# Attention scores as 32x32 tiles of TensorE in four PSUM banks, in a kernel of layer norm, attention, GRU and feed-forward

## The reference

```python
x = x + attn(cond(x, ...))                 # cond: block sums, softmax over 8 blocks, layer norm
# attn: 32 heads of size 8, causal, with a slope on the distance
scores = einsum('bhqd,bhkd->bhqk', q, k) / sqrt(8)
probs  = softmax(where(causal, scores, -10000) + alibi * m)
attn   = einsum('bhqk,bhkd->bhqd', probs, v) @ W_proj + b_proj
x = x + ffn(gru(cond_2048, x, ...))        # 32 steps of a GRU over the tokens
```

## Time and profile before

| | |
|---|---|
| time, median of 3 runs | 455.13 us (454.35 to 455.9) |
| time of the profiled execution | 453.68 us |
| its span | 451.9 us |
| PE busy | 430.9 us, 95% |
| DVE busy | 326.4 us, 72% |
| ACT busy | 247.0 us, 55% |
| POOL busy | 109.6 us, 24% |

### The profile page before, as it was taken

One profiled execution on the slowest core, in us unless ns is written; L12 is line 12 of the kernel. 1 busy time (PEld: TensorE's weight loads), 2 busy tenths in 40 slices (PEclk: granted clock), 3 DMA queues, 4 the chain that ended last, 5 costly groups with the idle time before them and its releaser, 6 DMA issues.

```text
span 451.9 us, 13521 instructions
## 1 busy us (share of the span) xinstructions
PE 430.9 (95%) x5470; PEld 354.6 (78%) x5470; DVE 326.4 (72%) x1008; ACT 247.0 (55%) x564; POOL 109.6 (24%) x127
## 2 busy tenths in 40 slices
PE   8899799999999999999999889899999999999994
PEld 5657587786877777778677779799999999999984
DVE  3656688697888886988867955657676677667665
ACT  6255648558485585674866653444444444444341
POOL 7422345424344453341544310000000000000000
PEclk9999999999999999999999999999999999999999
DMA  7802512424134142321312200001010101000002
GB/s 299 317 4 80 166 34 82 136 71 144 36 91 133 47 120 75 95 82 38 99 26 61 60 3 2 0 2 46 1 49 0 48 5 45 25 23 25 23 25 70
DMA packets 34268, 30.36 MB, mean 67 GB/s; under 512 B 4128, under 2 KB 29344, under 8 KB 34208
## 3 DMA queue, kind: packets, MB, share of 16 engines
q1 hardware_dynamic: 34208, 29.51, 20.9%
HBM read 16.91 MB, written 8.39 MB: 56 GB/s over the span
## 4 chain that ended last, share of the span: by engine, by line
PE 74%; DVE 14%; ACT 4%; issue 3%; DMA 2%; POOL 2%; SPq 1%; DVEq 0%; POOLq 0%; ACTq 0%
PE ps_a L1089 10%; PE ps_s L1234 7%; PE ps_t L1234 6%; PE ps_o L1234 6%; PE ps_s L1288 5%; PE ps_s L1138 5%; PE ps_m L1180 5%; PE ps_t L1288 4%; PE ps_a L1288 4%; PE ps_t L1151 4%; PE ps_m L1288 4%; PE ps_o L1162 3%; DVE mx L822 2%; PE ps_m L1172 2%; PE ps_a L1036 2%
## 5 line engine op out<-in xcount | busy, mean ns | idle before, releaser
L475 POOL TENSOR_TENSOR sc<-masked,mx 128x512 f32<-128x512 f32 x32 | 45.8, 1431 | 111.0 <-DVE mx L822 111.0
L1089 PE MATMUL ps_a<-yT_r,w_qkv_r 128*128 128x512 f32 x192 | 50.2, 406 | 1.6 <-POOL yT_r L449 1.2
L814 DVE COPY_PREDICATED masked<-kst,ps_s 128x512 f32<-128x512 int32 x64 | 43.9, 734 | 2.3 <-PE ps_s L1138 2.0
L1089 PEld LDWEIGHTS ps_a<-yT_r,w_qkv_r 128*128 128x128 f32 x192 | 34.6, 189 | 11.9 <-POOL yT_r L449 2.1
L676 ACT ACTIVATE zg<-ps_t,brz 128x128 f32<-128x128 f32 x64 | 20.1, 365 | 39.6 <-PE ps_t L1234 37.4
L574 ACT ACTIVATE sc<-sc 128x512 f32<-128x512 f32 x64 | 37.1, 621 | 7.1 <-DVE sc L828 5.6
L822 DVE TENSOR_REDUCE mx<-masked 128x16 f32<-128x512 f32 x64 | 40.4, 671 | 0.0
L952 DVE SCALAR_TENSOR_TENSOR rg<-ps_o,vec,rg 128x128 f32<-128x128 f32 x64 | 19.5, 348 | 24.9 <-PE ps_o L1234 24.0
L506 ACT ACTIVATE pT<-ps_t 128x512 f32<-128x512 f32 x64 | 34.9, 602 | 4.1 <-PE ps_t L1151 3.2
L1234 PEld LDWEIGHTS ps_s<-hT,w_hh 128*128 128x128 f32 x256 | 33.0, 191 | 4.8 <-DVE hT L970 2.8
L1180 PE MATMUL ps_m<-oT,w_p 128*128 128x128 f32 x256 | 35.3, 281 | 0.8 <-ACT oT L506 0.8
(11 more groups left out here) (128 smaller groups left out, 869.9 us busy)
## 6 DMA issues: line engine op xcount, KB each, us to landing
xf<-in_x_feat SPq DMA_DIRECT2D x8, 512.0 KB, 4.1
xg<-in_x_tok SPq DMA_DIRECT2D x8, 512.0 KB, 4.9
kbd<-kn SPq DMA_DIRECT2D x128, 32.0 KB, 1.9
v_dram<-vn SPq DMA_DIRECT2D x16, 256.0 KB, 3.1
vbd<-v_dram SPq DMA_DIRECT2D x64, 64.0 KB, 2.0
out_feat<-ost SPq DMA_DIRECT2D x16, 256.0 KB, 2.0
w_qkv<-in_wqkv SPq DMA_DIRECT2D x1, 768.0 KB, 7.6
w_ih<-in_wih SPq DMA_DIRECT2D x1, 768.0 KB, 10.4
```

The lines of the kernel that those rows point to most:

```text
L475: nc.gpsimd.tensor_tensor(shifted, kept, m.unsqueeze(2).to_broadcast([P, NH // 2, S]), ALU.subtract).then_inc(sc_sub[1], 1)
L814: nc.vector.copy_predicated(kept, keep.unsqueeze(1).to_broadcast([P, NH // 2, S]), ps_s[:, h * 512:(h + 1) * 512].rearrange("p (h k) -> p ...
L1089: last = nc.tensor.matmul(bank, w_qkv_r[a][:, c, first_col + m * P:first_col + (m + 1) * P], yT_r[b][:, c, :], start=(a == b == c == 0), s ...
```

## The change

It sets `RH = 4`, and so `KH = 4`. The scores of a tile are then 32 matmuls on sixteen tiles of 32x32, four groups of rows by four of columns, each with 128 columns of output; the keys are block-diagonal over four heads instead of eight, and `kbd` is half as large. Each of the four row groups has a PSUM bank of its own and fills half of it: two banks of `ps_s`, and two of `ps_u`, which has the place of `ps_t`. The transposed probabilities now go to `ps_s`. So the scores of tile n + 1 and the transposed probabilities of tile n share two banks, and `transpose_probs(n)` has a new wait for DVE's masked copy of half 0 of tile n + 1. PE's order changes so that other work stands between the scores and the transposes, and in step 1 ACT's copy of the first query chunk moves ahead of `attn_out`. The diff, cut to its core:

```diff
-RH = 2
+RH = 4
 KH = P // RH // 8
-            return {"r": ps_s, "z": ps_t, "n": ps_a}[which][:, m * 512:(m + 1) * 512]
+            return {"r": ps_u, "z": ps_s, "n": ps_a}[which][:, m * 512:(m + 1) * 512]
+        def score_banks(h):
+            return (ps_s, ps_u)[h][:, :].rearrange("p (r x) -> p r x", r=RH // 2)[:, :, 0:C * KH * S]
# ACT, tile_step
+                if i == 1 and not last_group:
+                    q_chunk(g + 1, 0)
                 if n > 0:
                     attn_out(n - 1)
...
                 if i == 1 and not last_group:
-                    q_chunk(g + 1, 0)
                     q_chunk(g + 1, 1)
# DVE, softmax_mask
-                    nc.vector.copy_predicated(kept, keep.unsqueeze(1).to_broadcast([P, NH // 2, S]),
-                                              ps_s[:, h * 512:(h + 1) * 512].rearrange("p (h k) -> p h k", k=S)
-                                              ).then_inc(sc_out, 1)
+                    kept = masked[:, h * 512:(h + 1) * 512].rearrange("p (r h k) -> p r h k", r=RH // 2, k=S)
+                    nc.vector.copy_predicated(
+                        kept, keep.unsqueeze(1).unsqueeze(1).to_broadcast([P, RH // 2, C * KH, S]),
+                        score_banks(h).rearrange("p r (h k) -> p r h k", k=S)).then_inc(sc_out, 1)
# PE, scores
+                if n >= 2:
+                    pe.wait_ge(pt_out, 2 * n - 2)
                 for c in range(C):
                     for r in range(RH):
                         rows = slice(r * P // RH, (r + 1) * P // RH)
+                        bank = score_banks(r // 2)[:, r % 2, c * KH * S:(c + 1) * KH * S]
                         for b in range(TB):
                             cols = slice(i * P + b * S, i * P + (b + 1) * S)
-                            out_cols = slice((r * C + c) * KH * S, (r * C + c + 1) * KH * S)
-                            last = nc.tensor.matmul(ps_s[b * S:(b + 1) * S, out_cols], qn[rows, g % 2, c, cols],
+                            last = nc.tensor.matmul(bank[b * S:(b + 1) * S, :], qn[rows, g % 2, c, cols],
                                                     kbd[rows, c, :, cols], start=True, stop=True,
                                                     tile_position=(r * P // RH, b * S))
# PE, transpose_probs
+                if n + 1 < NT:
+                    pe.wait_ge(sc_out, 2 * n + 3)
+                else:
+                    pe.wait_ge(pt_out, 2 * n)
                 for h in range(2):
                     pe.wait_ge(sc_exp, 2 * n + h + 1)
-                    if not first:
-                        pe.wait_ge(pt_out, 2 * n - 1 + h)
                     for q in range(HW):
                         col = (h * HW + q) * P
-                        last = nc.tensor.transpose(ps_t[:, col:col + P], sc[:, p, col:col + P], ident)
+                        last = nc.tensor.transpose(ps_s[:, col:col + P], sc[:, p, col:col + P], ident)
                     last.then_inc(pt_mm, 1)
# PE, tile_step
+                products_ahead = g + 3 < NG and i == 3
+                if n + 1 < NT:
+                    scores(n + 1, (n + 1) // GT, (n + 1) % GT)
                 if i == 0 and not last_group:
                     transpose_y(g + 1, norm_ahead and g > 0)
-                if n + 1 < NT:
-                    scores(n + 1, (n + 1) // GT, (n + 1) % GT)
-                if n > 0:
-                    transpose_attn(n - 1)
+                if i == 1 and not last_group:
+                    work_ahead(g + 1, 1, 0)
                 if norm_ahead and i == 2:
                     pe.wait_ge(q_out, 2 * g + 4)
                     spread_proj(g + 2, ps_a)
-                transpose_probs(n, n % 2, first=(n == 0))
+                if products_ahead:
+                    pe.wait_ge(v_out, 2 * g + 4)
+                    block_product(g + 3, ps_a[:, 0:512], 0)
+                if n > 0:
+                    transpose_attn(n - 1)
+                transpose_probs(n, n % 2)
```

More of the change, by code:

```diff
@@ L172, in adaln_attn_gru_ffn @@
         ps_s = ctx.enter_context(nc.psum_tensor("ps_s", [P, 1024], F32))
-        ps_t = ctx.enter_context(nc.psum_tensor("ps_t", [P, 1024], F32))
+        ps_u = ctx.enter_context(nc.psum_tensor("ps_u", [P, 1024], F32))
         ps_o = ctx.enter_context(nc.psum_tensor("ps_o", [P, 512], F32))
@@ L580, in probs_out @@
                     copy_out(pT[:, h * HW:(h + 1) * HW, :].rearrange("p q n -> p (q n)"),
-                             ps_t[:, h * 512:(h + 1) * 512]).then_inc(pt_out, 1)
+                             ps_s[:, h * 512:(h + 1) * 512]).then_inc(pt_out, 1)
             def attn_out(n):
@@ L806, in softmax_mask @@
             def softmax_mask(n, p, first=False):
-                for h, kept, _, _ in halves(p):
+                for h in range(2):
                     if not first:
@@ L883, in _ @@
             rest_of_proj(1, proj_ps_1)
-            add_proj(1, ps_t)
+            add_proj(1, ps_u)
             token_stats(1)
@@ L1129, in scores @@
                 pe.wait_ge(q_out, C * (g + 1))
-                if not first:
+                if first:
+                    pe.wait_ge(z_done, 4)
+                else:
                     pe.wait_ge(sc_out, 2 * n)
+                if n >= 2:
+                    pe.wait_ge(pt_out, 2 * n - 2)
                 for c in range(C):
@@ L1213, in _ @@
             work_ahead(0, 1, 0)
-            spread_proj(1, ps_t)
+            spread_proj(1, ps_u)
             work_ahead(0, 1, 1)
@@ L1260, in tile_step @@
                     cond_row(g + 2)
+                if i in (0, 2) and not last_group:
+                    work_ahead(g + 1, i, 0)
                 if i < 3 and not last_group:
-                    work_ahead(g + 1, i, 0)
                     work_ahead(g + 1, i, 1)
-                if g + 3 < NG and i == 3:
-                    pe.wait_ge(v_out, 2 * g + 4)
-                    block_products(g + 3, ps_a[:, 0:512])
+                if products_ahead:
+                    block_product(g + 3, ps_a[:, 0:512], 1)
                 if norm_ahead and i == 1:
```

6 lines of the change are left out of this document (3 added, 3 removed).

## The result

The changed kernel takes **461.07 us** (median, 460.78 to 461.25) against 455.27 for the kernel before on the same chip: ratio 1.0128, 95% interval 1.011 to 1.0147. It is slower by 5.8 us, where 451.1 was forecast, and outside the range. The profiled execution has a span of 459.2 us against 451.9.

A forecast was written before the change was run, and what follows sets the result against it. Bound by PE, then DVE in steps 2 and 3, then ACT 0.11 behind PE. Terms -0.42 - 2.94 + 0.35 - 0.55 - 0.45 = -4.0 took 455.13 to 451.1 us; range 446.5 to 455.3.

The forecast's parts named there:

- the size of the score block: All score matmuls of one tile of tokens on PE: 0.60 us instead of 1.02, saving 0.42 a block.
- 0.73 is an upper bound on what the issue costs: Issue of 64 PE instructions in a score block: at most 0.73 us, taken from `probs_v`.
- Start: First scores, on the chain with DVE waiting for them: -0.42 us.
- Step 1: Groups 0 to 6, PE sets the step and the new wait is hidden by 0.17: seven times -0.42, -2.94 us.
- Steps 2 and 3: Scores to end of transposes: 9.95 us against 9.88, the moved block product filling the saving; five groups, +0.35.
- The rival with a block of 1.02: Sixteen tiles no faster than eight, new wait stays: step 3's transposes end at 10.58 us, total 459.0; chance 0.09.
- Step 3 into 0: Groups 0 to 4: ACT's list of 6.57 us sets the start of `project_out`; five times -0.11, -0.55 us.
- End: After the last value projection DVE sets the pace and loses its waits for scores: -0.45 us.
- SP: Key load queue: half as many loads let the save go up to 1.0 us earlier; counted as nothing.
- The masked copy: DVE's copy reading two banks keeps its 0.64 us; 0.1 more on DVE's part would cost 0.2 a group.
- third rival: Score block keeps 1.02 us on sixteen tiles and the new wait stays: +3.9, 459.0 us; chance 0.09.
- if PE's denser instructions arrive late: Sign that the forecast would be wrong, on PE's instruction supply; no size given.

The follow-up runs named there:

- e12: Kernel before, each score matmul cut in two of 128 columns, a tile taken up again only after the other seven: 458.89 us, ratio 1.0075.
- e6: Changed kernel, each score matmul reading 64 of its 128 key columns from the third tile on: 456.59 us (one run).
- e9: Changed kernel, each score matmul reading 32 of its 128 key columns from the third tile on: 455.91 us (one run).
- e8: Changed kernel, score block in two halves, one ahead of the earlier tile's `probs_v` and one behind it: 467.24 us, ratio 1.0255.
- e3: Changed kernel, `transpose_y`, half projection, `spread_proj` and block product moved ahead of the scores: 478.69 us, ratio 1.0502.
- e13: Changed kernel, tile order in a sweep turned, column groups outside and row groups inside: 461.47 us, ratio 1.0133.
- e14: Changed kernel, second sweep taking the row groups as 1, 0, 3, 2: 461.24 us, ratio 1.0121.
- e4: Changed kernel, half of the score matmuls left out from tile 2 on, so the output is not the reference's: 451.41 us, ratio 0.9913.
- e2n: Kernel before with the new order of PE and ACT alone, old tiles and banks, no new wait: 457.21 us, ratio 1.0057.
- e2: Kernel before with the new wait and the new order of PE and ACT, old 64x32 tiles and banks: 461.3 us, ratio 1.0117.
- e5: Kernel before, each score matmul cut into four of 64 columns, run one after the other on the same tile: 555.3 us (one run).
- e1: Kernel before with only the new wait for the next tile's masked copy ahead of the transposes: 470.77 us, ratio 1.0333.

## Why the prediction was wrong

**The step that failed is the size of the score block**: "I take 0.60, since its working reproduces the block of before", with the bound under it, "0.73 is an upper bound on what the issue costs". The block is 4 x 0.109 + 0.57, not + 0.16. The constant was read from eight tiles, where it is 0.16 with 16 matmuls (1.02 - 0.86) and 0.22 with 32 (e12), and carried over to sixteen. The bound is none either: `probs_v` runs on four tiles and with 40 columns. PE's timeline of a block of the changed kernel shows where the rest is:

```profile
128.88 0.34 PE L1148 MATMUL ps_s<-kbd,qn 32*32 32x128 f32 x8
128.94 0.34 PE L1148 MATMUL ps_u<-kbd,qn 32*32 32x128 f32 x8
129.00 0.34 PE L1148 MATMUL ps_s<-kbd,qn 32*32 32x128 f32 x8
129.07 0.32 PE L1148 MATMUL ps_u<-kbd,qn 32*32 32x128 f32 x8
129.18 0.52 PE L1148 MATMUL ps_s<-kbd,qn 32*32 32x128 f32 x9
129.43 0.29 PE L1148 MATMUL ps_u<-kbd,qn 32*32 32x128 f32 x1
129.43 0.27 PE L1148 MATMUL ps_s<-kbd,qn 32*32 32x128 f32 x1
129.44 0.29 PE L1148 MATMUL ps_u<-kbd,qn 32*32 32x128 f32 x1
...
129.54 0.40 PE L1148 MATMUL ps_u<-kbd,qn 32*32 32x128 f32 x9
```

The first four rows are the first sweep: sixteen tiles start in 0.12, some 7 ns apart, and all of them their second instruction in the next 0.13. The tiles do run side by side. Then comes the second sweep, and it is unlike the first. One by one in the trace: the 32nd start is at 0.246 from the block's first, the 33rd at 0.30, the 34th, that tile's second instruction, a full 0.11 later at 0.41; from there the first instructions of the other fifteen tiles come 16.6 ns apart, and their second ones between them (the alternation of ps_u and ps_s in the last rows). The last start is at 0.79 and the next instruction of PE at 0.99. In e6 and e9 the spacing is 16.6 ns too, with a half and a quarter of the columns. A pause of 0.16 and fifteen starts at 16.6 instead of 7 ns (0.14) are 0.30 of the 0.41 by which the constant was too small. In e8, where `probs_v` stands between the sweeps, both are like the first.

**Why a second sweep right behind the first is slower stays open.** It is not what stands ahead (e3), the order of the tiles or the reuse of one (e13, e14). What e12 does not exclude is the number of instructions in the block. Its starts within a sweep over eight tiles come 7 ns apart up to the 36th, and from the 37th on (0.48 from the first) mostly 17 ns apart, as here; on eight tiles that costs little, since a sweep lasts one pass of 0.109 anyway. Where a block has 32 instructions (before, e4, e8) no such spacing shows. In both kernels PE's weight loads halt behind the 33rd of the block's 64. Against this rival speaks `probs_v`, whose 64 instructions keep a mean spacing of 9.5 ns. No run separates a sweep over tiles taken up again from a long block.

TensorE: Matmul & The Clock Gate of the Trainium skill, Part 1, has about 25 ns between starts as a floor, however few columns a matmul has. With starts 7 ns apart on sixteen tiles the trace disagrees, as it did with `probs_v`.

Point by point:

- **Start, -0.42.** Came to +0.35 in these two traces: the first block of scores is 0.25 shorter for DVE but starts 0.60 later, 40.01 against 39.41. The later start is in part scatter: in PE's timeline it is at 39.94 here, at 39.38 in e9 and 39.34 before.
- **Step 1, -0.42 each.** +0.02. PE sets the step, and no wait shows in it, as reasoned; the saving was not there. In e4, with a block shorter by 0.56, it is 0.23, and the wait that was to be hidden takes part of the rest.
- **Steps 2 and 3, +0.07 each.** From step 2's scores to the end of step 3's transposes: 151.63 to 161.31 + 0.87 = 162.18, so 10.55 against 9.88, +0.67. The rival with a block of 1.02 had 10.58. The order alone (e2n) loses 0.57 here: with a block of 1.02 ahead of it, the moved block product makes PE the later one.
- **Step 3 into 0.** The 6.57 of ACT's list came out exactly, at 131.21 + 0.87 to 138.65. But it is no gain of 0.11 once the transposes themselves are later.
- **End, -0.45.** The last two groups lost 3.5. Of that the stop and the low clock behind it are 2.5 in the last two steps (6.85 and 4.38 where e2 has 4.68 and 4.02), if e2's are taken as what they would be without.
- **SP.** Eight issues in 10.82 us for sixteen in 13.09, and no wait for keys or values. Nothing, as counted.
- **The masked copy** from two banks takes 0.72 to 0.74, as in the earlier trace rows.

```profile
233.34 10.82 SPq L341 DMA_DIRECT2D kbd<-kn  x8
```

The third rival ("sixteen tiles are no faster than eight, and the new wait stays") is what happened in its block, steps and total: it said 459.0, and 461.1 less 2.5 is 458.6. The reason it gave for the block, that four groups of rows do not run side by side, is not what the timeline shows, so its 1.02 is right by luck. It had a chance of 0.09, too little. Against it I held that two row groups run side by side, which says nothing about a second sweep; and `probs_v` in 0.73 was the only row near the new form, 64 instructions on four tiles.

**The stop.** The prediction named it as a risk ("if PE's denser instructions arrive late") and gave it no price. In the timeline:

```profile
262.05 0.35 PE L1148 MATMUL ps_u<-kbd,qn 32*32 32x128 f32 x6
...
264.28 0.41 PE L1148 MATMUL ps_u<-kbd,qn 32*32 32x128 f32 x3 [1.88 <-issue]
...
265.76 1.79 PE L1193 MATMUL ps_m<-oT,w_p 128*128 128x128 f32 x8
267.49 1.30 PE L1175 MATMUL ps_o<-vbd,pT 128*32 128x40 f32 x64
```

Behind the stop, `project_out` and `probs_v` are slow as well, 1.79 and 1.30 where they take 1.06 and 0.80. That is the clock and not the code. PE had stood still from 262.40 to 264.28, and 1.6 us after it went on the granted clock fell to 1.2 GHz for 3.4 us. The row gives the stretch, its length, the busy time of PE, PEld, DVE, ACT and POOL, the granted clock, the DMA share and GB/s:

```profile
265.90:269.30 3.40, 2.88 (x73) 2.50 (x71) 2.64 (x7) 1.98 (x4) 1.43 (x1) 0.50 0.02 5
```

In the chain the two take 1.63 and 1.27 there, against 0.89 and 0.73 one step earlier: 1.3 us more, besides the 1.9 of the stop. Ten of the eleven traces with such a stop (the changed kernel, e3, e5, e6, e8 to e14) have a stretch of 3.4 or 6.8 us at 1.2 GHz that begins within 1.8 us of a stop's end, all but e12; before, e1, e2, e2n and e4 have neither stop nor such a stretch in the last group. That the stop brings the low clock on is the likely reading; no run separates the two.

The queue that carries instructions moves one packet between 261.5 and 262 us, just ahead of the stop. That the engine waits there for its own code is the reading that fits the places some 252 apart, the packet, and the density: the change gives PE 64 more recorded instructions a tile, 2,048 in all, and in the last group a step has only 4.6 us. e12 has it with that number on the old tiles; the kernels with the old number (before, e1, e2, e2n), and e4, show no such stop at the end. No run removes it from the changed kernel, so its worth of some 2.5 us, low clock included, is read from the steps of e2 alone. The same queue has eight packets fewer before the change, 43: one for every 256 of the 2,048 instructions. The first line is of the changed kernel, the second of the kernel before:

```profile
q8 instruction: 51, 0.84, 0.8%
q8 instruction: 43, 0.70, 0.7%
```

Runtime: NRT & Kernel Launch of the Trainium skill, Instruction fetch mechanics, says that an engine's code comes in blocks of 16 KiB or 256 instructions while the block before it runs, and that this is mostly hidden. The rows above agree on the size (0.84 MB in 51 packets, 16 KB each) and on the number, as the places of the stops do; here, in dense code, it is not always hidden.

## What to carry to other kernels

A measured block splits into a part that scales and a constant, and only the first may be carried to another tiling; the constant must be measured in the new form, or be given the range of everything that could hide in it. Price the precondition of a change before its gain: here the wait that the shared banks ask for cost 14.8 us alone, and the order that covers most of it costs 2.2 by itself. A change that adds many instructions to an engine is to be charged in the stages where its steps are shortest. And two equal totals (e2 and the change, e4 and the forecast) prove little until their steps are compared.

## What the runs showed of the hardware

- Sixteen 32x32 tiles of TensorE start their matmuls about 7 ns apart in one sweep and overlap. Behind the 32nd instruction of a block of 64 the next start comes 0.055 us later, the one behind it a whole pass later (0.110, 0.056, 0.032 us for 128, 64, 32 columns), and from there the tiles' first instructions come 16.6 ns apart, whatever the columns (the changed kernel, e6, e9). On eight tiles (e12) a spacing of 17 ns begins with the 37th.
- Consecutive matmuls on one tile hold up the other tiles queued behind them: with four in a row (e5), eight instructions of 64 columns take 0.254 us where their own tile needs 0.45, and 128 take 4.36; 64 instructions of 128 columns, all tiles in turn, took 1.09 (e12).
- PE stopped for 1.3 to 2.5 us where its code was dense, at places that are 193 to 195 of PE's records beyond a multiple of 256, and the place moved with the code and not with the work.
- In ten of eleven traces with such a stop, TensorE's granted clock fell to 1.2 GHz for 3.4 or 6.8 us, beginning within 1.8 us of a stop's end. In the changed kernel `project_out` then took 1.63 us in place of 0.89.
